# Layer-1 operands and down-weight transposes moved into the product stage, the first maximum by a diagonal, the gate matmul's first wait shortened

## The reference, cut to what matters

```
x = x + tanh(g_xattn[0]) * attn0(layernorm(x), ctx)             # one head, 256 wide
x = x + tanh(g_ffn[0])   * ffn0(layernorm(x))
x = x + tanh(g_xattn[1]) * attn1(layernorm(x), ctx, mask)       # 16 heads, relative bias, output projection
x = x + tanh(g_ffn[1])   * moe1(layernorm(x))                   # 8 experts, one per token

def ffn0(x):                       # quantised; act_qdq needs the maximum over the WHOLE tensor
    x    = act_qdq(x)
    up   = act_qdq(x @ dequant(w_up).T)                         # 256 -> 768
    gate = act_qdq(x @ dequant(w_gate).T)
    sig  = fixed_qdq_u16(sigmoid(gate))
    gate = act_qdq(gate * sig)
    o    = act_qdq(gate * up)
    return o @ dequant(w_down).T                                # 768 -> 256

act_qdq(x) = round(x / s) * s, s = max|x| / 32767
```

## Time and profile before

| | |
|---|---|
| median of 3 runs | 571.54 us (570.98 to 571.58) |
| profiled execution | 572.57 us, of it span 570.8 us |
| TensorE clock granted over the span | 0.889 of full speed |
| busy | PE 452.1, DVE 338.5, ACT 255.7, POOL 126.7 us |

### The profile page before, as it was taken

One profiled execution on the slowest core, in us unless ns is written; L12 is line 12 of the kernel. 1 busy time (PEld: TensorE's weight loads), 2 busy tenths in 40 slices (PEclk: granted clock), 3 DMA queues, 4 the chain that ended last, 5 costly groups with the idle time before them and its releaser, 6 DMA issues.

```text
span 570.8 us, 7978 instructions
## 1 busy us (share of the span) xinstructions
PE 452.1 (79%) x2430; PEld 298.2 (52%) x2431; DVE 338.5 (59%) x724; ACT 255.7 (45%) x460; POOL 126.7 (22%) x148
## 2 busy tenths in 40 slices
PE   4788659998993002989799999999996269999993
PEld 3676524453441001878566666666664136677672
DVE  1289676335999699335456655666546814554552
ACT  1326335546884784400456645556454133234310
POOL 4125236103000000010576000100010173443222
PEclk9985669998998555999899999999999569999998
DMA  8800000000000001000019900000007031112000
GB/s 243 223 2 1 2 0 2 0 0 0 0 0 1 0 0 44 1 1 1 1 32 373 374 2 1 2 2 0 1 1 219 5 94 51 53 53 60 25 26 1
DMA packets 27226, 27.04 MB, mean 47 GB/s; under 512 B 11570, under 2 KB 23391, under 8 KB 26944
## 3 DMA queue, kind: packets, MB, share of 16 engines
q1 hardware_dynamic: 24992, 21.57, 11.8%
q0 software_dynamic: 2208, 5.14, 3.1%
HBM read 22.48 MB, written 5.15 MB: 48 GB/s over the span
## 4 chain that ended last, share of the span: by engine, by line
PE 64%; DVE 13%; issue 13%; ACT 5%; POOL 2%; DMA 1%; DVEq 1%; SPq 1%; POOLq 0%; ACTq 0%
PE bank L1413 51%; PE bank L1636 6%; PE bank L1460 3%; PE bank L1782 2%; DVE big_g L1144 2%; PE bank L1654 1%; ACT big_u L733 1%; DVE stat L972 1%; DVE amU L1156 1%; DVE amZ L1150 1%; ACT yT L733 1%; POOL rstd L591 1%; DVE x_rows L1046 1%; DMA gates<-in_g_ffn 1%; DVE tmp L1139 1%
## 5 line engine op out<-in xcount | busy, mean ns | idle before, releaser
L1413 PE MATMUL bank<-yT,ffn_w 128*128 x192 | 86.8, 615 | 7.6 <-ACTq L791 7.0
L1413 PE MATMUL bank<-ffn_w,big_u 128*128 128x256 f32 x192 | 43.8, 390 | 49.1 <-ACT big_u L733 49.0
L1413 PEld LDWEIGHTS bank<-yT,ffn_w 128*128 128x128 f32 x192 | 37.8, 198 | 55.4 <-issue 54.2
L1413 PEld LDWEIGHTS bank<-ffn_w,big_u 128*128 128x128 f32 x192 | 37.4, 196 | 55.4 <-ACT big_u L733 49.9
L733 ACT ACTIVATE big_u<-bank 77x512 f32<-77x512 f32 (+4 forms) x103 | 58.2, 579 | 16.4 <-PE bank L1636 10.2
L1257 DVE TENSOR_REDUCE mx<-bank 128x4 f32<-128x308 f32 x64 | 30.6, 479 | 44.5 <-PE bank L1413 44.5
L894 ACT ACTIVATE big_g<-big_g 128x308 f32<-128x308 f32 x64 | 29.4, 459 | 46.2 <-DVE big_g L1258 46.2
L1413 PE MATMUL bank<-k_blockdiag,big_g 128*128 128x308 f32 x128 | 45.7, 442 | 0.7 <-ACT yT L733 0.7
L1413 PE MATMUL bank<-big_g,yT 128*128 x92 | 44.2, 625 | 0.7 <-issue 0.7
L1413 PE MATMUL bank<-big_u,yT 128*128 x184 | 41.8, 380 | 1.6 <-DVE yT L1376 1.6
L733 ACT ACTIVATE yT<-bank 128x256 f32<-128x256 f32 (+1 forms) x47 | 17.5, 419 | 54.2 <-PE bank L1460 44.3
(11 more groups left out here) (258 smaller groups left out, 807.6 us busy)
## 6 DMA issues: line engine op xcount, KB each, us to landing
big_g<-in_L_ffn_W SPq DMA_DIRECT2D x1, 4096.0 KB, 16.9
big_u<-in_L_ffn_W SPq DMA_DIRECT2D x1, 4096.0 KB, 26.5
x_rows<-in_x SPq DMA_DIRECT2D x2, 1024.0 KB, 7.4
ffn_w<-in_L_ffn_b SPq DMA_DIRECT2D x1, 2048.0 KB, 24.3
tmp<-bias_by_distance SPq DMA_DIRECT2D x2, 616.0 KB, 5.0
token_rows<-x_rows SPq DMA_DIRECT2D x1, 1032.0 KB, 7.3
tmp<-in_L_ffn_b SPq DMA_DIRECT2D x1, 1024.0 KB, 5.2
token_rows<-x_rows SPq DMA_DIRECT2D x1, 774.0 KB, 9.3
```

Source lines behind the costliest of these rows:

```text
L1413: return pe.matmul(out_, lhsT=lhsT, rhs=rhs, start=first, stop=last)
```

## The change

- **First maximum.** POOL's `all_max(MX)` goes. DVE multiplies the identity by the partition maxima (`diag`, 128 x 128), PE multiplies a matrix of ones with it into bank 3, so that every partition holds all 128 maxima, and DVE takes the maximum over the row.
- **Gate's first wait.** ACT raises `gu_sb` before its four copies of `YT`, so the gate matmul of quarter 0 waits for `nq` of quarter 0 alone.
- **Between gate and up.** Only the 12 transposes of the up weights stay, in banks 6, 7 and 0; they wait for the first block of the last quarter to be copied, not for the last. The sigmoid table is loaded in the gate product's last quarter.
- **After the up product.** PE's `layer1_operands` comes here, with the down weights' 12 transposes and, new, a second transpose of the context, since ctx, Wk, Wv, bv and w_red of layer 1 are now loaded late, into the space of the gate and up weights, by five DMAs that SP issues once PE has finished the up product (`gu_ps` 48). ACT's copies of down weights and context stand before its wait for `scal_z`; those of the router and the values after its product stage.
- **DVE.** The router weight's three small operations and the six of the mask stand between its two maxima after the up product and its wait for `MZ`. The keys' ten stand after the quantising of stage 6, ahead of the down product's additions.
- **POOL.** `gap`, `keepv`, `keep` stand after MG and wait for `gu_ps` 48; `KBD` stands after MP. SP's load of B1 waits for `KBD`.
- The second sigmoid buffer lies elsewhere in `TMP`, so that the down weights survive the up product.

The diff, cut to its core:

```diff
@@ buffers
-        expand = part(BIGU, 10880, [H, D])
+        expand = sb("expand", [H, D])
+        diag = sb("diag", [P, P])
-        sig = part(TMP, 2 * HF, [P, 2, HF])
+        sig = TMP[:, :].rearrange("p (a b) -> p a b", a=2)[:, :, HF:2 * HF]
+        CTXL = part(FW, 0, [KEYS, NB, D])
+        WK1 = part(FW, 512, [P, CH, D])
+        WV1 = part(FW, 1024, [P, CH, D])
...
@@ sync
-            sp.dma_start(WK1, chunks(a["L1_xattn_Wk"])).then_inc(s.ld_l1, 16)
-            sp.dma_start(WV1, chunks(a["L1_xattn_Wv"])).then_inc(s.ld_l1, 16)
...
             sp.dma_start(ext_d, ext).then_inc(s.ext_stored, 16)
+            sp.wait_ge(s.gu_ps, 2 * FJ * NQB)
+            sp.dma_start(CTXL, a["ctx_1024"].rearrange("b k d -> k b d")).then_inc(s.ld_late, 16)
+            sp.dma_start(WK1, chunks(a["L1_xattn_Wk"])).then_inc(s.ld_late, 16)
+            sp.dma_start(WV1, chunks(a["L1_xattn_Wv"])).then_inc(s.ld_late, 16)
+            sp.dma_start(bv1, row(a["L1_xattn_bv"])).then_inc(s.ld_late, 16)
+            sp.dma_start(WR, chunks(a["L1_ffn_w_red"])).then_inc(s.ld_late, 16)
...
@@ gpsimd
-            pool.tensor_copy(gap, keep8[:, :])
-            pool.tensor_scalar(keepv[:, :], keepc8[:, :], -1.0, 1.0, ALU.mult, ALU.add)
-            pool.tensor_scalar(keep, keep8[:, :], -1.0, 1.0, ALU.mult, ALU.add).then_inc(s.keep_sb, 1)
-            all_max(MX)
             quantised(1, 0)
...
             all_max(MG)
-            [KBD: wait k1_sb, four tensor_tensor, then_inc kbd_sb]
+            pool.wait_ge(s.gu_ps, 2 * FJ * NQB)
+            [gap, keepv, keep, then_inc keep_sb]
             all_max(MZ)
             all_max(MU)
             all_max(MP)
+            [KBD]
@@ scalar
+            act.sem_inc(s.gu_sb, FJ)
             for q in range(NQB):
                 copy(YT[:, :, q * QB:(q + 1) * QB], ..., s.tq_y, q + 1, s.nq, bias=-MAGIC)
-            act.sem_inc(s.gu_sb, FJ)
...
-                if q == 2:
-                    act.wait_ge(s.wq_sb, 3)
+                if q == 3:
+                    act.activation(warm[:, :], warm[:, :], ACT.Sigmoid)
                 for j in range(FJ):
                     gate_out(q, j)
-            [6 copies of FW, V1 x2, WRT, WGNT, GM, warm Sigmoid]
+            for g in range(3):
+                copy(FW[:, g * 512:(g + 1) * 512], pb[(6, 7, 0)[g]], s.wT_ps, 3 + g + 1, s.wT_sb)
             [sigmoid stage]
+            for g in range(3):
+                copy(FW[:, (6 + g) * 512:(7 + g) * 512], pb[g], s.wT_ps, 6 + g + 1, s.wT_sb)
+            copy(CTXLT, pb[3][:, 0:2 * NB * KEYS].rearrange("p (c n) -> p c n", c=CH), s.ctxL_ps, 1, s.ctxL_sb)
             act.wait_ge(s.scal_z, 1)
             [product stage]
+            [WRT, WGNT, wait keepv_sb, V1 x2]
             [ints]
+            [GM]
@@ vector
-            dve.tensor_reduce(sc[:, 0:1], amY[:, :], AX.X, ALU.max).then_inc(s.am_sb, 1)
+            c.link(dve.tensor_reduce(sc[:, 0:1], amY[:, :], AX.X, ALU.max))
+            dve.tensor_scalar(diag[:, :], ident[:, :], sc[:, 0:1], None, ALU.mult).then_inc(s.am_sb, 1)
             dve.wait_ge(s.ar_sb, MX)
+            c.link(dve.tensor_reduce(sc[:, 1:2], pb[3][:, 0:P], AX.X, ALU.max))
...
             dve.tensor_reduce(sc[:, 6:7], amU[:, :], AX.X, ALU.max).then_inc(s.am_sb, 1)
+            [wnorm: 3 operations; wait keep_sb; keep: 6 operations, then_inc keepv_sb]
             dve.wait_ge(s.ar_sb, MZ)
...
+            [keys: 10 operations, then_inc k1_sb]   # behind the 8 of L1199
             scalar(21, sc[:, 19:20], ALU.mult, tg[:, 2:3])
@@ tensor
             y2_in(NT // 4 - 1)
+            pe.wait_ge(s.am_sb, MX)
+            mm(pb[3][:, 0:P], ones[:, :], diag[:, :], True, True).then_inc(s.ar_sb, 1)
...
                 if n:
-                    layer1_operands()
+                    pe.wait_ge(s.wq_sb, 3)
+                    pe.wait_ge(s.gu_sb, FJ + FJ * NQB - FJ + 1)
+                    for g in range(3):
+                        weightsT(g, pb[(6, 7, 0)[g]])
+                    pe.wait_ge(s.wT_sb, 6)
                 [24 blocks]
+            def layer1_operands():
+                pe.wait_ge(s.gu_sb, FJ + 2 * FJ * NQB)
+                for g in range(3):
+                    weightsT(6 + g, pb[g])
+                pe.wait_ge(s.ld_late, 16 * 5)
+                [4 transposes of CTXL into pb[3], then_inc ctxL_ps; head scales; wait ctxL_sb]
+                [keys; values; router: wait wrT_sb, wgn_sb; transpose; wait wgT_sb; 4 matmuls]
+            layer1_operands()
+            pe.wait_ge(s.wT_sb, 9)
```

More of the change, by code:

```diff
@@ L108, in __init__ @@
         self.wq_sb = sem("wq_sb")
+        self.ld_late = sem("ld_late")
+        self.ctxL_ps = sem("ctxL_ps")
+        self.ctxL_sb = sem("ctxL_sb")
         self.wT_ps = sem("wT_ps")
@@ L361, in flamingo_kernel @@
         bk1 = sb("bk1", [P, CH])
-        bv1 = part(BIGU, 10304, [1, D])
+        bv1 = part(FW, 1536, [1, D])
+        CTXLT = part(FW, 1824, [P, CH, NB * KEYS])
         bo1 = sb("bo1", [P, D])
@@ L368, in flamingo_kernel @@
         keep8 = sb("keep8", [P, NB * KEYS], U8)
-        keep = part(BIGU, 10560, [P, NB * KEYS])
-        K1T = sb("k1T", [P, CH, NB * KEYS])
+        keep = part(FW, 2388, [P, NB * KEYS])
+        K1T = part(FW, 0, [P, CH, NB * KEYS])
         KBD = sb("k_blockdiag", [P, NB * CH * 8, KEYS])
@@ L378, in flamingo_kernel @@
         kmean = sb("kmean", [P, CH, NB])
-        gap = part(BIGU, 11424, [P, NB * KEYS])
-        fill = part(BIGU, 11584, [P, CH, NB * KEYS])
+        gap = part(FW, 2542, [P, NB * KEYS])
+        fill = part(FW, 2696, [P, CH, NB * KEYS])
         mrow = part(BIGU, 10720, [1, NB * KEYS])
@@ L395, in flamingo_kernel @@
         mx = sb("mx", [P, 2, HQ])
-        WR = part(BIGU, 11136, [P, CH, G])
-        WRT = part(BIGU, 11168, [G, D])
+        WR = part(FW, 1792, [P, CH, G])
+        WRT = part(FW, 2132, [G, D])
         wg = sb("wg", [E, G])
@@ L656, in _ @@
             all_max(MG)
+            pool.wait_ge(s.gu_ps, 2 * FJ * NQB)
+            pool.tensor_copy(gap, keep8[:, :])
+            pool.tensor_scalar(keepv[:, :], keepc8[:, :], -1.0, 1.0, ALU.mult, ALU.add)
+            pool.tensor_scalar(keep, keep8[:, :], -1.0, 1.0, ALU.mult, ALU.add).then_inc(s.keep_sb, 1)
+            all_max(MZ)
+            all_max(MU)
+            all_max(MP)
             pool.wait_ge(s.k1_sb, 1)
@@ L783, in _ @@
                     y2T_out(g - 1)
-            act.wait_ge(s.ld_l1, 16 * 14)
+            act.wait_ge(s.ld_l1, 16 * 10)
             act.activation(els[:, :], ls[:, :], ACT.Exp).then_inc(s.els_sb, 1)
@@ L842, in _ @@
                                    scale=sc[:, 17:18]).then_inc(s.nzu_done, 1)
+            copy(WRT, pb[6][0:G, 0:D], s.l1_ps, WRT_, s.wrT_sb)
+            copy(WGNT[:, :], pb[6][0:G, D:D + E], s.l1_ps, WGT_, s.wgT_sb)
+            act.wait_ge(s.keepv_sb, 1)
+            for b in range(NB):
+                copy(V1[:, b * H:(b + 1) * H, 0:HD], pb[5][0:KEYS, b * D:(b + 1) * D].rearrange("p (n d) -> p n d", d=HD),
+                     s.l1_ps, V1S, s.v1_sb, scale=keepv[:, b:b + 1])
             def ints(q):
@@ L862, in _ @@
                 ints(q)
+            copy(GM[:, :, 0:E], pb[7][:, 0:CH * E].rearrange("p (c e) -> p c e", c=CH), s.l1_ps, GMS, s.gm_sb)
             for q in range(NQB):
@@ L1199, in _ @@
                 dve.tensor_scalar(b, b, sc[:, 20:21], MAGIC, ALU.mult, ALU.add).then_inc(s.tq_p, 1)
+            dve.wait_ge(s.l1_ps, K1)
+            c.link(dve.tensor_copy(cscale[:, :], pb[4][:, 0:CH]))
+            for ci in range(CH):
+                c.link(dve.tensor_scalar(K1T[:, ci, :], pb[4][:, 2 + ci * NB * KEYS:2 + (ci + 1) * NB * KEYS],
+                                         bk1[:, ci:ci + 1], cscale[:, ci:ci + 1], ALU.add, ALU.mult))
+            c.link(dve.tensor_tensor(K1T[:, :, :], K1T[:, :, :], keep.unsqueeze(1).to_broadcast([P, CH, NB * KEYS]),
+                                     ALU.mult))
+            c.link(dve.tensor_reduce(kmean[:, :, :], K1T[:, :, :].rearrange("p c (b k) -> p c b k", b=NB), AX.X, ALU.add))
+            c.link(dve.tensor_tensor(kmean[:, :, :], kmean[:, :, :], rkeep[:, :].unsqueeze(1).to_broadcast([P, CH, NB]),
+                                     ALU.mult))
+            for ci in range(CH):
+                c.link(dve.tensor_tensor(fill[:, ci, :].rearrange("p (b k) -> p b k", b=NB),
+                                         gap.rearrange("p (b k) -> p b k", b=NB),
+                                         kmean[:, ci, :].unsqueeze(2).to_broadcast([P, NB, KEYS]), ALU.mult))
+            dve.tensor_tensor(K1T[:, :, :], K1T[:, :, :], fill, ALU.add).then_inc(s.k1_sb, 1)
             scalar(21, sc[:, 19:20], ALU.mult, tg[:, 2:3])
@@ L1427, in _, with keysT @@
             ins.then_inc(s.wq0T_ps, 1)
-            def keysT(ps, w, done):
+            def keysT(ps, w, ctx, done):
                 for dj in range(CH):
@@ L1443, in _ @@
             pe.wait_ge(s.ctxT_sb, 1)
-            keysT(pb[2], WK0, s.k0_ps)
-            values(pb[4], WV0, bv0, s.v0_ps)
```

(6 more changed lines are left out.)

128 lines of the change are left out of this document (43 added, 85 removed).

## The result

| | median (runs) | profiled execution, span |
|---|---|---|
| before, in the changed kernel's group | 571.56 (570.98 to 571.92) | 572.57, 570.8 |
| changed | 558.09 (557.31 to 558.76) | 557.82, 556.1 |
| forecast | 554.8 (551.8 to 558.2) | 555.9 |

The ratio is 0.9756 with an interval of 0.9734 to 0.9778. The time lies inside the range, near its upper end. So 2.0 us of the miss lie in the two traces, and 1.3 us in which execution had been profiled.

A forecast was written before the change was run, and what follows sets the result against it. Chain of waits: TensorE's matmuls 64%, DVE 13%, no recorded work 13%. Terms 4.0 + 9.6 + 2.0 - 1.2 + 2.3 = 16.7 took the profiled 572.57 to 555.9, median 554.8, range 551.8 to 558.2.

The forecast's parts named there:

- diagonal and early count: Before the gate: maximum without POOL 2.9 us, shorter first wait 1.1 us; together 4.0, bounds 3.4 to 6.5.
- gate's end to sigmoid: Between gate and up product: ACT's first sigmoid work comes at 124.6 instead of 134.23, 9.6 us off.
- first half of the sigmoid stage: Up product's first quarter at clock 1.00: DVE's second rounding 7.8 us after first sigmoid work, gain 2.0, bounds 0 to 2.1.
- MZ: After the up maxima: nine small DVE operations take 1.8 us, 0.59 of it formerly idle; costs 1.2 us.
- down: Down product: PE's 1.99 us wait and 0.4 us of slower transposes go; gain 2.3, bounds 2.0 to 2.4.
- the switch waits for `gu_ps` too: Before MZ's reduction: two POOL switches follow each other, 2.5 us in place of 1.2; 556.1, within a shared chance of 0.08.
- dear form: At MZ: a reduction pays its switch after its operand, adding 6.1 us; 560.9, within a shared chance of 0.08.
- The slower side: Product stage: late loads block ACT; from 30 us of landing slower than before; chance 0.04, half of it slower.
- A: Up product starts cold again, so the 2.0 us gain goes: 556.8; chance 0.09.
- A': The gate product starts warm: 552.8; chance 0.07.
- C: After the up maxima: DVE's small operations stall beside POOL, -4 in place of -1.2: 557.6; chance 0.07.
- E: Between gate and up: an overlooked order keeps PE or DVE waiting; half of 11.6 us comes back: 560.6; chance 0.05.

The follow-up runs named there:

- b_front: The kernel before with only the first maximum by the diagonal and ACT's count ahead of its copies; 566.94 us, ratio 0.9899.
- a_late_count: The changed kernel with ACT's count put back behind its four copies of the transposed rows; 559.42 us against the changed kernel's 558.13.
- b_busy: The kernel before with seven unread bf16 matmuls in PE's wait between gate and up product; 572.82 us, ratio 0.9988.
- b_switch: The kernel before with one tiny ordinary POOL operation behind MP's reduction, asking for the way back earlier; 570.03 us, ratio 0.9944.
- a_early_switch: The changed kernel with one tiny ordinary POOL operation right behind MG's reduction; 555.75 us, ratio to before 0.9699.
- a_again: The changed kernel run once more with nothing changed, as a second look; 558.13 us, ratio to before 0.9752.
- a_warm_experts: The changed kernel with the mask's work ahead of the gate and filler matmuls in PE's waits, also ahead of the experts; 550.79 us, ratio to before 0.9621.

## Why the prediction was right, and where its sum was off

By its own steps, from the profiled pair:

| step | forecast | traces | verdict |
|---|---|---|---|
| diagonal and early count | 4.0 | 3.57 | right (2.7 and 0.85, shown by b_front and, as a difference, a_late_count) |
| gate's end to sigmoid | 9.6 | 9.53 | right (13.17 to 3.64, from the end of the gate's last matmul, 121.06 and 116.95); no run has it alone |
| first half of the sigmoid stage | 2.0 | 1.76 | right, and its cause shown by b_busy |
| MZ | -1.2 | -3.03 | **mis-sized**: POOL's switches |
| down | 2.3 | 2.16 | right, shown by b_switch |
| rest | 0 | 0.71 | maxima of layer 0 0.29 earlier, gate 0.25 shorter, 0.17 behind |
| sum | 16.7 | 14.70 | |

The five steps together are 2.7 short; 0.7 came back from what the forecast had at nothing, and that was luck: the end of layer 0's maxima alone lies between 69.12 and 71.01 in the traces of these kernels. The measured 558.09 lies only 0.1 inside the range.

**The step that was off** is the one on POOL's configuration: "after MG back to ordinary (free, 50 us)". The rule in it held: a switch cost 5.6 to 8.1 us from its own place and was free where that much waiting followed. The place was wrong. I took any ordinary operation to ask for the switch, and the trace of before had none that told a copy from the rest. The copy ran in either configuration (at 160.94 in the reduction's, at 162.43 in a_early_switch in the ordinary one), so both switches landed behind the wait for PE, and MZ cost 3.03 us where the forecast had 1.2. The rival that I had priced for this, "the switch waits for `gu_ps` too", put the reduction 2.5 us after the end of the maxima; in this trace it stands 3.08 behind them (172.50 to 175.58), and ends the wait of DVE that the nine operations (1.73) no longer fill. It had 0.08 together with its dear form. The forecast should have asked what the first instruction behind each switch point is, and whether it needs the switch at all.

The dear form of that rival, which was the reading of the Trainium skill (GPSIMD Engine Reference, section 2.1, Instruction dispatch) as a price net of the wait for the event, is ruled out here: in a_early_switch the first reduction after a switch started 0.14 after its operand (L1151, ended 173.91) and 0.05 after the last maximum. As to size, that section of the Trainium skill says about 6 us, and the runs show 5.6 to 6.1 from the instruction to the reduction and 6.7 to 8.1 on the way back.

**The slower side** needed loads that land 30 us late. The last landed 4.7 us after the first issue at 160.9. Late weights cost nothing because ACT stood idle for 10.7 us behind its copy. ("Five times the bytes" in the prediction is six times, 4096 KB against 682.) Of the other rivals, A did not occur (clock 1.00 into the up product), nor A' (the gate began at 0.50), nor C (DVE's nine operations took 1.73 us, forecast 1.8), nor E (the up product started 2.45 behind the gate's end, forecast 2.4).

**From profile to median**: I carried the 1.03 by which the profiled execution of before lay above its median over to the changed kernel. There it was -0.3. With executions of one kernel up to 4 us apart (before: 570.4 to 574.7 over one group), one profiled execution doesn't fix a median to 1 us, and the range should have had that term.

## What to carry to other kernels

Read what an engine was doing at each of its switch points, and ask which instruction really causes the switch: a switch of 5.6 to 8.1 us is free where the engine would wait anyway, and two in a row behind one late semaphore are not. When a wait in front of a matmul stage is removed, count the clock as well as the wait, and where the wait can't be removed, cheap matmuls in it can give part of the stage back, if they reach to its end: a burst that stopped 2.88 us early was followed by one that overshot. Compare stages by differences within a trace when the time of a kernel scatters by more than the effect.

## What the runs showed of the hardware

- A CAST on POOL ran straight away in the reduction's configuration (160.94), while a TENSOR_SCALAR behind it came 7.92 us later. The switch to the reduction took 5.6 us (changed kernel) to 6.1 (before) from its instruction, the one back 6.7 (a_early_switch) to 8.1 (a_again).
- The granted clock of PE followed bf16 filler of a matrix of ones. It was 0.50 at the start of the burst of 20 that began at 200.6 and 1.00 before its end, and the fp32 stage behind it ran at 1.00 from its first matmul. In a_warm_experts, where PE had nothing from 65.13 to 68.00, the clock fell to 0.50 and a burst of 9 took 4.05 us instead of 2.11.
- The stretch at 0.50 at the head of the gate product is not the same in each execution, with the same code around it: the changed kernel had 0.75 at 77 to 78 and 1.00 from there in one trace (gate from 73.52), 0.63 at 78 to 79 in the other (gate from 74.00), and a_early_switch, whose gate also starts at 74.00, stood at 0.50 until 80.
